# Convolution taps that read the projection in its PSUM bank, and two more injections on GpSimd

## The reference

```python
x = x + gnn(layernorm(x), adj, ...)      # attention weights adj*exp(leaky_relu(..)), 3 hops, relu
x = x + ffn(layernorm(x), ...)           # x @ W_fc1 + b, mamba block, @ W_fc2 + b

# the mamba block, per sequence of L = 128 steps, 1024 inner channels, 16 states
u, z = split(h @ W_in.T)
u_pad = pad(u, 3 zeros in front)
u = silu(sum(u_pad[:, k:k+L, :] * conv_w[:, k] for k in range(4)) + conv_b)
dt, B, C = split(u @ W_xproj.T)
delta = softplus(dt @ W_dt.T + b_dt);  A = -exp(A_log)
h_t = exp(delta_t * A) * h_(t-1) + (delta_t * u_t) * B_t       # the scan, for 16 states
y = (sum over states of h_t * C_t + u * D) * silu(z)
out = y @ W_out.T
```

## Time and profile before

| | |
|---|---|
| median of 3 runs | 4181.41 us |
| lowest, highest | 4177.37, 4192.95 us |
| profiled execution | 4176.09 us |
| its span in the profile | 4174.3 us |
| mean granted clock of TensorE | 0.961 of full speed |
| busy: PE, DVE, ACT, POOL | 3575.7, 3766.7, 2976.9, 3326.2 us |

### The profile page before, as it was taken

The page is one execution under the profiler, slowest core; times in us unless marked ns, Lnnn a source line. Parts: engine busy times, 40 slices in busy tenths (PEclk is TensorE's granted clock), DMA queues, the critical chain, the costliest instruction groups (busy, mean ns, idle before and its releaser), DMA issues.

```text
span 4174.3 us, 45057 instructions
## 1 busy us (share of the span) xinstructions
PE 3575.7 (86%) x11386; PEld 2016.6 (48%) x11386; DVE 3766.7 (90%) x3219; ACT 2976.9 (71%) x6358; POOL 3326.2 (80%) x1764
## 2 busy tenths in 40 slices
PE   6688889888888888889888888888889888888887
PEld 3454555444545444545444445444545444555443
DVE  0399999999999999999899999999999999999998
ACT  1577777777777777777777777777777777777764
POOL 0287878888888888888888888888878888788888
PEclk9799999999999999999999999999999999999999
DMA  2111001111101111101111101111101111101110
GB/s 96 47 50 53 36 29 43 50 52 52 39 25 44 49 52 52 52 12 43 50 52 52 52 12 44 49 52 52 51 12 43 50 52 52 39 25 43 46 46 8
DMA packets 50716, 183.79 MB, mean 44 GB/s; under 512 B 7339, under 2 KB 33203, under 8 KB 42067
## 3 DMA queue, kind: packets, MB, share of 16 engines
q1 hardware_dynamic: 48880, 174.17, 11.0%
q10 hardware_dynamic: 1636, 7.83, 0.5%
HBM read 164.15 MB, written 17.83 MB: 44 GB/s over the span
## 4 chain that ended last, share of the span: by engine, by line
PE 32%; DVE 23%; ACT 19%; issue 17%; POOL 6%; DVEq 1%; DMA 0%; ACTq 0%; POOLq 0%; SPq 0%
PE y_ps L699 15%; DVE st L891 11%; ACT dec L467 8%; PE d_ps L751 4%; DVE st L879 4%; POOL st L404 4%; DVE u L912 3%; PE y_ps L695 3%; PE d_ps L762 2%; ACT L467 2%; PE d_ps L739 2%; PE d_ps L773 2%; DVE zs L898 2%; ACT delta L550 1%; ACT zs L522 1%
## 5 line engine op out<-in xcount | busy, mean ns | idle before, releaser
L404 POOL TENSOR_TENSOR st<-st,bc 128x1024 f32<-128x1024 f32 x1024 | 2403.4, 2356 | 642.7 <-DVE u L912 373.5
L891 DVE TENSOR_TENSOR_SCAN st<-dec,st 128x1024 f32<-128x1024 f32 x1024 | 2327.5, 2279 | 176.9 <-ACT dec L467 174.9
L467 ACT ACTIVATE dec<-delta,decay 128x254 f32<-128x254 f32 x4096 | 1700.6, 467 | 797.1 <-DVE st L891 791.1
L699 PE MATMUL y_ps<-st,ident 128*128 128x512 f32 x4096 | 2023.1, 624 | 242.3 <-POOL st L404 237.3
L699 PEld LDWEIGHTS y_ps<-st,ident 128*128 128x128 f32 x4096 | 770.2, 197 | 1025.9 <-issue 612.6
L879 DVE TENSOR_TENSOR st<-du,bc 128x1024 f32<-128x1024 f32 x800 | 963.5, 1204 | 36.2 <-ACT du L453 35.9
L388 POOL TENSOR_TENSOR st<-du_sb,bc 128x1024 f32<-128x1024 f32 x224 | 528.6, 2360 | 0.1
L912 DVE SCALAR_TENSOR_TENSOR u<-upad,chan,u 128x256 f32<-128x256 f32 x768 | 392.3, 551 | 6.4 <-ACT u L513 6.4
L695 PE MATMUL y_ps<-u,diag 128*128 128x256 f32 x512 | 157.6, 434 | 209.7 <-DVE zs L898 209.7
L751 PE MATMUL d_ps<-xnT,wxz 128*128 128x256 f32 x1024 | 254.7, 393 | 62.9 <-ACT zs L522 62.2
L751 PEld LDWEIGHTS d_ps<-xnT,wxz 128*128 128x128 f32 x1024 | 198.3, 196 | 161.7 <-ACT zs L522 103.3
(11 more groups left out here) (105 smaller groups left out, 2831.2 us busy)
## 6 DMA issues: line engine op xcount, KB each, us to landing
bc<-bc_dram SPq DMA_DIRECT2D x64, 2048.0 KB, 9.6
xg<-x_dram SPq DMA_DIRECT2D x32, 256.0 KB, 2.8
x_dram<-xg SPq DMA_DIRECT2D x32, 256.0 KB, 2.0
last_x<-x_dram SPq DMA_DIRECT2D x32, 256.0 KB, 2.6
out_dram<-last_x SPq DMA_DIRECT2D x32, 256.0 KB, 2.2
bc<-w_inT_dram ACTq DMA_DIRECT2D x1, 4096.0 KB
adjt<-adjT_dram SPq DMA_DIRECT2D x32, 128.0 KB, 2.5
bc<-w_out_dram ACTq DMA_DIRECT2D x1, 2048.0 KB
```

The costliest lines, as they stand in the source:

```text
L404: nc.gpsimd.tensor_tensor(st[:, sl, :, :, :], st[:, sl, :, :, :], bc[:, p, 1, SU * q:SU * q + SU, None, :].to_broadcast([P, SU, 2, T]), AL ...
L467: a = nc.scalar.activation(dec[:, v % 2, s, j, :].rearrange("p (b t) -> p b t", b=PAIR)[:, :, 1:], delta[:, p, 2 * i + j, :].rearrange("p ...
L699: mm = nc.tensor.matmul(y_all, ident[:, :], st[:, sl, s, :, :].rearrange("p j t -> p (j t)"), start=False, stop=(q == Q - 1 and s == SU - ...
L891: nc.vector.tensor_tensor_scan(h, dec[:, v % 2, :, :, :].rearrange("p s j t -> p (s j t)"), h, 0.0, ALU.mult, ALU.add).then_inc(S["scanned ...
```

## The change

The taps read the projection where TensorE put it, in d_ps, and add to u in SBUF; a tap late by n steps of time writes only the columns from n on, so no padding is needed. upad, its memset and ACT's copies into it are gone. The projection's bias is now missing from the taps; for the columns from 3 on it is part of the constant bconv, and the first three columns of each sequence get a correction (edge, computed once) in one tensor_tensor a group, at the step after the last projection's taps begin. The projection of a pair now waits for the six taps of the pair before. GpSimd's product no longer waits for taps. GpSimd injects nine units, with 4 and 12 new, and some of its other steps move. SiLU of u is at step 13. The fold of wo moves to the body before the first scan, in y_ps, copied out by DVE. X_STEPS, DT_STEPS, EXP_STEPS and LN_STEP name steps that were numbers before; their values are the same.

```diff
-POOL_UNITS = (0, 8, 16, 20, 24, 27, 30)
-POOL_INJECTS = {5: 8, 13: 16, 17: 20, 20: 24, 24: 27, 26: 30}
-POOL_DELTAS = {2: 1, 9: 2, 11: 3}
-POOL_DUS = {4: 1, 12: 2, 18: 3}
+POOL_UNITS = (0, 4, 8, 12, 16, 20, 24, 27, 30)
+POOL_INJECTS = {0: 4, 5: 8, 8: 12, 12: 16, 16: 20, 20: 24, 23: 27, 26: 30}
+POOL_DELTAS = {2: 1, 9: 2, 14: 3}
+POOL_DUS = {4: 1, 11: 2, 18: 3}
-U_STEPS = (0, 2, 4, 7)
+U_STEPS = (0, 3, 6, 9)
-SILU_U, SILU_Z = 14, 6
+SILU_U, SILU_Z = 13, 6
-FOLD_OUT = {9: 0, 10: 3, 11: 1, 13: 2}
+FOLD_OUT = (1, 4, 7, 10)
+CONV = (TAPS - 1) * J + 1
...
                 wait(pool, "scanned", U * k + v + 1)
-                if dense and 2 <= v < 2 + (TAPS - 1) * JP:
-                    wait(pool, "taps", (TAPS - 1) * J * (k + 1) + 2 * (v - 2) + 2)
...
                     wait(act, "u_mm", J // 2 * g + i + 1)
-                    wait(act, "taps", (TAPS - 1) * (J * g + (2 if i == 3 else 0)))
...
                     for j in (2 * i, 2 * i + 1):
-                        nc.scalar.activation(upad[:, j % UPADS, :, TAPS - 1:],
-                                             d_ps[:, j % 2, :].rearrange("p (b t) -> p b t", b=PAIR),
-                                             ACT.Identity, bias=bxz[:, j:j + 1])
                         nc.scalar.activation(u[:, r, j, :], d_ps[:, j % 2, :], ACT.Identity, bias=bconv[:, j:j + 1],
                                              scale=chan[:, TAPS - 1, j:j + 1]).then_inc(S["u_biased"], 1)
...
-                        wait(pe, "u_biased", J * g + 2 * i)
+                        wait(pe, "taps", CONV * g + 6 * i)
...
+            def conv(dve, g, r, v):
+
+                for i, start in enumerate(U_STEPS):
+                    for n in range(6):
+                        if v == start + 1 + n // 3:
+                            tap(dve, g, r, i, n)
+                if v == U_STEPS[3] + 2:
+
+                    wait(dve, "taps", CONV * (g + 1) - 1)
+                    first = u[:, r, :, :].rearrange("p j (b t) -> p j b t", b=PAIR)[:, :, :, 0:TAPS - 1]
+                    nc.vector.tensor_tensor(first, first, edge[:, :, None, :].to_broadcast([P, J, PAIR, TAPS - 1]),
+                                            ALU.add).then_inc(S["taps"], 1)
+
+            def tap(dve, g, r, i, n):
+
+                m, j, late = n // 2, 2 * i + n % 2, TAPS - 1 - n // 2
+                if m == 0:
+                    wait(dve, "u_biased", J * g + 2 * i + 2)
+                else:
+                    wait(dve, "taps", CONV * g + 6 * i + n - 1)
+                dst = u[:, r, j, :].rearrange("p (b t) -> p b t", b=PAIR)[:, :, late:]
+                src = d_ps[:, j % 2, :].rearrange("p (b t) -> p b t", b=PAIR)[:, :, 0:L - late]
+                nc.vector.scalar_tensor_tensor(dst, src, chan[:, m, j:j + 1], dst, ALU.mult, ALU.add)\
+                    .then_inc(S["taps"], 1)
```

More of the change, by code:

```diff
@@ L87, in build @@
         bconv = sb("bconv", [P, J])
+        edge = sb("edge", [P, J, TAPS - 1])
+        part = sb("part", [P, TAPS - 1, J])
         c0 = sb("c0", [P, 2])
@@ L350, in body @@
                     if scan:
-                        c_product(pool, k, p, v, steps, dense)
+                        c_product(pool, k, p, v, steps)
                         if v in POOL_DELTAS:
@@ L390, in inject, with c_product @@
                                         ALU.mult).then_inc(S["p_injected"], 1)
-            def c_product(pool, k, p, v, steps, dense):
+            def c_product(pool, k, p, v, steps):
                 if v == 0:
@@ L437, in fold_out @@
                     nc.scalar.activation(decay[:, :, :], s_alog, ACT.Exp).then_inc(S["decay_exp"], 1)
[L439 to L447, removed]
             def copy_du(act, k, p, i):
@@ L524, in dense_act @@
                 if v == SILU_U:
-                    wait(act, "taps", (TAPS - 1) * (J * g + J))
+                    wait(act, "taps", CONV * (g + 1))
                     nc.scalar.activation(u[:, r, :, :], u[:, r, :, :], ACT.Silu).then_inc(S["silu_u"], 1)
-                if v == 17:
+                if v - 1 == X_STEPS[1]:
                     wait(act, "proj_mm", g + 1)
@@ L650, in fold_wo @@
                     return
[L651 to L658, removed]
+                m = FOLD_OUT.index(v)
+                wait(pe, "wo_folded", m)
                 for j in range(2):
                     for c in range(HC):
-                        mm = nc.tensor.matmul(dst[:, j * DIM:(j + 1) * DIM],
+                        mm = nc.tensor.matmul(y_all[:, j * DIM:(j + 1) * DIM],
                                               s_wout[:, c, (2 * m + j) * P:(2 * m + j + 1) * P], s_fc2T[:, c, :],
@@ L674, in body @@
                         fold(pe, v)
-                    if isinstance(k, int) and k == 0:
+                    if dense and not scan:
                         fold_wo(pe, v)
@@ L753, in dense_pe @@
                     mm.then_inc(S["z_mm"], 1)
-                if v in (15, 16):
-                    h = v - 15
+                if v in X_STEPS:
+                    h = X_STEPS.index(v)
                     if h == 0:
                         wait(pe, "silu_u", g + 1)
-                        if isinstance(g, int) and g == 1:
-                            pe.wait_ge(S["wo_folded"], JP)
                     for j in range(4 * h, 4 * h + 4):
@@ L764, in dense_pe @@
                         mm.then_inc(S["proj_mm"], 1)
-                if v in (18, 20, 22, 24):
-                    m = (v - 18) // 2
+                if v in DT_STEPS:
+                    m = DT_STEPS.index(v)
                     if m == 0:
@@ L866, in _ @@
             nc.vector.memset(halfs[:, :], -0.5).then_inc(S["memsets"], 1)
-            nc.vector.memset(upad[:, :, :, :], 0.0).then_inc(S["memsets"], 1)
             dve.wait_ge(S["w_graph"], 16 * len(GRAPH_LOADS))
@@ new lines, in conv_constants @@
+            def conv_constants(dve):
+                dve.wait_ge(S["bias_loaded"], 16)
+                for m in range(TAPS - 1):
+                    nc.vector.scalar_tensor_tensor(part[:, m, :], bxz[:, 0:J], -1.0, chan[:, m, :], ALU.mult, ALU.mult)\
+                        .then_inc(S["edge_part"], 1)
+                nc.vector.tensor_tensor(bconv[:, :], bxz[:, 0:J], chan[:, TAPS - 1, :], ALU.mult)\
+                    .then_inc(S["edge_part"], 1)
+                dve.wait_ge(S["edge_part"], 4)
+                nc.vector.tensor_copy(edge[:, :, 2], part[:, 0, :])
+                nc.vector.tensor_tensor(edge[:, :, 1], part[:, 0, :], part[:, 1, :], ALU.add).then_inc(S["edge_part"], 1)
+                nc.vector.tensor_tensor(bconv[:, :], bconv[:, :], chan[:, TAPS, :], ALU.add).then_inc(S["edge_part"], 1)
+                dve.wait_ge(S["edge_part"], 6)
+                nc.vector.tensor_tensor(edge[:, :, 0], edge[:, :, 1], part[:, 2, :], ALU.add).then_inc(S["edge_part"], 1)
+                dve.wait_ge(S["edge_part"], 7)
+                nc.vector.tensor_tensor(bconv[:, :], bconv[:, :], edge[:, :, 0], ALU.subtract)\
+                    .then_inc(S["bconv_made"], 1)
@@ L915, in graph_dve, with fold_wo @@
+            def fold_wo(dve, v):
+                if v - 1 in FOLD_OUT:
+                    m = FOLD_OUT.index(v - 1)
+                    wait(dve, "wo_mm", m + 1)
+                    nc.vector.tensor_copy(wo[:, 2 * m:2 * m + 2, :].rearrange("p j d -> p (j d)"), y_all)\
+                        .then_inc(S["wo_folded"], 1)
             def graph_dve(dve, g, v, late):
@@ L990, in body @@
                     if dense:
-                        tap(dve, k + 1, r, v)
+                        conv(dve, k + 1, r, v)
+                    if dense and not scan:
+                        fold_wo(dve, v)
                     for g, _, ph in steps:
```

36 lines of the change are left out of this document (14 added, 22 removed).

## The result

The changed kernel takes 4335.9 us (median of 4 runs, 4330.3 to 4343.8) beside 4179.8 for the kernel before in the same runs: a ratio of 1.038, 95% interval 1.036 to 1.040. It is 156 us slower. The forecast was slower by 69 us, 4245, with a range from 4130 to 4305.

What follows compares the result with a forecast made beforehand. DVE was taken to bound the kernel: its program plus its waits set a body's time. Terms summed to +2.1 us a body, 65 over 31 bodies, plus 4 at the start: 4176 + 69 = 4245 us, range 4130 to 4305.

Steps and rivals of the forecast that it cites:

- the gate at v=18: GpSimd's backlog at v=13 to 15 shrinks, and with it DVE's gate waits; -0.4 us a body (0 to -1.0).
- Injections and taps: Two injections fewer on DVE, -2.26 us a body; taps reading PSUM escape contention with GpSimd, -2.06.
- D: Rival, chance 0.02: PSUM taps still collide with GpSimd, which never stands aside; +11.7 us a body, over 4600 us.
- The loop through d_ps: Taps follow ACT's copy without slack, so DVE stalls at v=4 (+2.5 us a body) and v=7 (+2.9).
- v=4: DVE waits for ACT's u copy: 1.7 us, 1.7 more in the other body with TensorE's low clock; mean +2.5.
- v=7: DVE waits for ACT's copy behind the SiLU of z: 9.4 against 6.6 us, a stall of 2.9 a body.
- Three steps of slack: Claim that the pipeline between ACT's copy and the taps had three steps of slack before and none after.
- A: Rival, chance 0.18: copies come in time and both stalls (5.4 us a body) stay away; faster, 4078 us.
- B: Rival, chance 0.14: no change, only one of the stalls opens; 4168 us without v=4, 4155 without v=7.
- The edge: Edge addition at v=11 waits 1.2 us for GpSimd's product of unit 11 and takes about 0.2; cost 1.4 a body.
- The last scans: DVE's scans of units 29 and 31 late in the body: no term in the sum, taken as 0.
- rival C: Rival, chance 0.12: DVE's stalls idle TensorE, its clock falls, projection late for v=10; 1.7 us a body more, 4298 us.

Runs made afterwards that it cites:

- e2: Changed kernel with all six taps of a projection in one step, two after the projection, giving ACT's copy a whole step more: 4157.8 us, ratio 0.995.
- e8: Changed kernel with ACT's SiLU of z at step 8 in place of 6: 4243.4 us, ratio 1.014.
- e9: Changed kernel with only GpSimd's injection of unit 16 back at step 13 in place of 12: 4242.5 us, ratio 1.015.
- e3: Kernel before with nine GpSimd units (4 and 12 added, injected at v=0 and v=8), taps as before: 4201.4 us, ratio 1.004.
- e4: Changed kernel with all of GpSimd's tables as in the kernel before (seven units): 4274.7 us, ratio 1.023.
- e6: Changed kernel, injections of 16, 20, 27 at their old steps, taps a step later, GpSimd's product of unit 11 waiting for the edge: 4059.5 us, ratio 0.970.

## Why the prediction was wrong

The direction, the place of the bound and most terms held; the size was half of the truth, and the time lay 31 us above the range. The step that failed is the gate at v=18: with that term as measured, the sum comes to 4326 us.

*Injections and taps* (-4.3): held, -4.2. The taps escape the port by reading PSUM: in the changed kernel no tap was long, with GpSimd free to run beside all of them.

```profile
L898 DVE SCALAR_TENSOR_TENSOR u<-d_ps,chan,u x768: 447/469/479, 125.5 to 4156.5; 128x250 f32<-128x250 f32 x64, 128x254 f32<-128x254 f32 x64, 128x252 f32<-128x252 f32 x64
```

The 1.6 us a body that the Trainium skill's cycle formula (VectorE: DVE Perf Modes, The TRN2 errata) would have added for a PSUM source isn't there: the median is 469 ns, and it was 473 from SBUF. D is out.

*The loop through d_ps* (+5.4): held, 4.9, and both stalls where they were walked; e2 and e8 show the cause. At v=4 the walk gave 1.7 in one body and 3.4 in the next, with TensorE at its low clock; the trace has 1.6 in 17 of the 27 bodies and 3.3 in 10. For v=7 the walk's own numbers, 9.4 less 6.6, give 2.8, not 2.9. "Three steps of slack" between ACT's copy and the taps was one step for the first pair, two for the second and three for the others. A and B are out.

*The edge* (+1.4): too small. I gave it the rest of one product after three taps. The taps end 1.2 us after the scan, but GpSimd began the product of unit 11 about then, behind its work for v=10, so the edge waited for nearly all of it. At 2.1 us it is nearer the upper bound, 2.6, than the 1.4.

*The gate at v=18* (-0.4, found +2.2): this is the step that failed, with the wrong sign. I wrote that GpSimd's backlog at v=13 to 15 shrinks because the injection of 16 comes a step earlier. Earlier meant ahead of the product of 13. The prediction doesn't follow TensorE's queue from there to the gate: TensorE has two halves of the x projection and a transposition between the sums of 13 and 15, in order, and the chain starts at product 13. e9 moves that one injection, takes the wait from 2.9 to 0, and the time to 4242.5.

*The last scans* (0, found +1.2): the sum had no term for them and gave no reason. ACT makes the decays of unit 29 after the logarithm of the softplus, and that after it has copied TensorE's first z projection, for which it waits. That projection in a body of the kernel before with a full clock, and in the changed kernel:

```profile
1166.79 1.13 PE L695 MATMUL y_ps<-u,diag 128*128 128x256 f32 x4 [2.47 <-DVE zs L898]
1167.75 1.88 PE L699 MATMUL y_ps<-st,ident 128*128 128x512 f32 x4
1169.47 1.89 PE L751 MATMUL d_ps<-xnT,wxz 128*128 128x256 f32 x8
```

```profile
2260.30 1.45 PE L677 MATMUL y_ps<-u,diag 128*128 128x256 f32 x4 [2.47 <-DVE zs L873]
2261.55 3.30 PE L681 MATMUL y_ps<-st,ident 128*128 128x512 f32 x4
2264.68 1.89 PE L731 MATMUL d_ps<-xnT,wxz 128*128 128x256 f32 x8
```

With the same idle time of 2.47 us ahead, the z projection starts 2.68 us after the gate's release in the one and 4.38 in the other, 1.7 later; the scan of unit 29 waits 2.62 and 4.32. The granted clock in these stretches is 1.00 and 0.60, and the mean over the run went from 0.961 to 0.926. So something like rival C's price came, but not at v=10, where the taps wait for nothing. That DVE's stalls lower the clock, as C had it, isn't shown: the wait for unit 29 is 4.3 in all 27 bodies of the changed kernel and about 4 in 18 of the 27 before, but e3, with no stall in the convolution, has a mean of 4.2 too, at a mean clock of 0.949, while e4, with both stalls, has 3.6. No run here controls the clock alone, and the cause stays open.

The walk of one body was good wherever I followed every engine to the wait. It was wrong at the gate and the edge, where I didn't follow GpSimd's queue and what waits behind it, and at the last scans, which I didn't walk.

## What to carry to other kernels

When a buffer that decouples two engines is taken away, count the steps between producer and consumer in the written order: here one step of the schedule was worth 178 us, and the work saved (4.2 us of DVE's a body in injections and taps) only showed once it was back. A step moved earlier in an in-order queue is moved ahead of something; follow what it now delays to the last waiter, with all that queues there. Work moved onto GpSimd pays only if DVE's two-operand SBUF work doesn't meet it, so the two edits have to be priced together.

## What was not expected of the hardware

An addition of 48 elements takes 0.21 us alone and 2.1 us beside GpSimd. The Trainium skill (SBUF - State Buffer, Who interferes with whom) gives the rule: a VectorE instruction with two SBUF inputs contends with a GpSimd instruction that reads SBUF. The trace agrees. That the wait is close to a whole product, in 30 of 32 cases, comes from where both engines stand in the schedule. In the kernel before, all 157 taps that take over 0.5 us run beside a record of GpSimd, and they end 0.28 us (the median) after that record does. And the share of time at the low clock changed with edits that leave TensorE's products as they are: the mean granted clock was 0.926 in the changed kernel, 0.974 in e6.
